# Loading the second copy of batch 0's coordinates on ScalarE's DMA queue, ahead of the mask

## The reference, cut to what matters

```python
def reference(x, ctx_4096, fside, mask, lora_B, router_W, router_b, Wq, ..., ln_b):
    # layer 0, with lora_A = ctx_4096 (4 x 64 x 512)
    w = softmax(x @ router_W.T + router_b)                 # 8 experts
    a_sum = einsum('bsh,arh->bsr', x, ctx_4096)
    x = nan_to_num(x + 0.5 * einsum('bsn,bsnh->bsh', w, einsum('bsr,nhr->bsnh', a_sum, lora_B)))
    # layer 1: x attends to ctx_4096, 32 heads of 16, masked where mask == 0
    Q, K, V = x @ Wq.T + bq, ctx @ Wk.T + bk, ctx @ Wv.T + bv
    x = layernorm(x + softmax(mask(Q K^T / 4)) V @ Wo.T + bo) * ln_g + ln_b
    # layers 2 and 3, the same: xyz = ctx_4096 (b, 64, 512), points = x
    sq = sum(xyz * xyz, axis=1)
    d2 = sq[:, :, None] + sq[:, None, :] - 2.0 * einsum('bdn,bdm->bnm', xyz, xyz)
    idx = top_k(-d2, 8)
    for i in range(4):
        p = leaky_relu(points)
        points = (fside[i] @ p + sum over the 8 neighbours of fside[i] @ p) / 9 + points
    return points
```

## Time and profile before

| | |
|---|---|
| median of 3 runs | 377.51 us (377.25, 377.51, 379.73) |
| the profiled execution, own time | 377.08 us |
| its span, first to last instruction | 375.3 us |
| PE busy | 365.6 us (97%) |
| PE weight loads | 309.9 us (83%) |
| DVE, ACT, POOL busy | 272.7, 176.9, 128.9 us |
| bytes moved by DMA | 22.47 MB |
| granted TensorE clock, mean | 1.000 |

### The profile page before, as it was taken

How to read it: one execution, slowest core, us unless ns; L and a number is a source line. 1 busy time by engine, 2 the same in 40 slices (tenths; PEclk the granted TensorE clock), 3 DMA queues, 4 the chain that set the end, 5 groups by cost and what they waited for, 6 DMA issues and landing times.

```text
span 375.3 us, 6566 instructions
## 1 busy us (share of the span) xinstructions
PE 365.6 (97%) x2396; PEld 309.9 (83%) x2396; DVE 272.7 (73%) x427; ACT 176.9 (47%) x308; POOL 128.9 (34%) x125
## 2 busy tenths in 40 slices
PE   7899999999999999999999999999999999999996
PEld 4677887878878877877898889898989889898895
DVE  4945899997899898579848984567686476565524
ACT  2256457857897586383426162234324233424311
POOL 5059216200501414023344254435427234344320
PEclk9999999999999999999999999999999999999999
DMA  6995127127038507500000000000000000000023
GB/s 198 325 347 164 22 65 186 39 53 161 8 102 190 68 2 149 69 0 3 2 1 0 2 0 2 0 2 1 2 0 2 0 2 0 3 0 2 0 86 140
DMA packets 25056, 22.47 MB, mean 60 GB/s; under 512 B 9537, under 2 KB 20546, under 8 KB 25026
## 3 DMA queue, kind: packets, MB, share of 16 engines
q1 hardware_dynamic: 24352, 22.04, 22.2%
q10 hardware_dynamic: 674, 0.02, 0.1%
HBM read 12.35 MB, written 3.15 MB: 41 GB/s over the span
## 4 chain that ended last, share of the span: by engine, by line
PE 85%; DVE 5%; ACT 4%; DMA 3%; issue 2%; SPq 1%; DVEq 0%; ACTq 0%
PE slot L564 82%; DMA wk<-in_WkT 3%; ACT k_blk_hi L943 2%; PE slot L684 1%; PE slot L693 1%; SPq L448 1%; PE slot L725 1%; ACT probT L976 1%; DVE p_full L1321 1%; DVE points L1331 1%; ACT adj L874 1%; DVE inv_full L1267 0%; ACT L976 0%; DVE stats L1282 0%; DVE shift L1255 0%
## 5 line engine op out<-in xcount | busy, mean ns | idle before, releaser
L1065 POOL TENSOR_TENSOR p_lo<-p_full,p_hi 128x512 fp32r<-128x512 f32 x64 | 86.0, 1361 | 157.1 <-ACT p_hi L1016 157.0
L1026 ACT ACTIVATE u_hi<-slot 128x512 fp32r<-128x512 f32 x64 | 36.1, 593 | 69.3 <-PE slot L564 69.2
L1326 DVE TENSOR_TENSOR u_lo<-slot,u_hi 128x512 fp32r<-128x512 f32 x64 | 42.4, 684 | 31.5 <-ACT u_hi L1026 31.5
L1016 ACT ACTIVATE p_hi<-p_full 128x512 fp32r<-128x512 f32 x64 | 39.0, 627 | 55.3 <-DVE p_full L1321 55.2
L564 PE MATMUL slot<-adj,u_hi 128*128 128x512 f32 x256 | 64.8, 392 | 0.1
L564 PE MATMUL slot<-fs_hi,p_hi 128*128 128x256 f32 x256 | 64.8, 286 | 0.0
L1331 DVE SCALAR_TENSOR_TENSOR points<-slot,points 128x512 f32<-128x512 f32 x64 | 42.7, 684 | 30.4 <-PE slot L564 30.4
L564 PE MATMUL slot<-adj,u_lo 128*128 128x512 f32 x256 | 64.1, 391 | 0.0
L564 PE MATMUL slot<-fs_lo,p_hi 128*128 128x256 f32 x256 | 64.1, 283 | 0.0
L1321 DVE SCALAR_TENSOR_TENSOR p_full<-points 128x512 f32<-128x512 f32 x64 | 54.3, 863 | 8.9 <-POOL p_lo L1065 6.3
L564 PEld LDWEIGHTS slot<-adj,u_lo 128*128 128x128 f32 x256 | 47.5, 188 | 10.1 <-issue 0.4
(11 more groups left out here) (144 smaller groups left out, 567.3 us busy)
## 6 DMA issues: line engine op xcount, KB each, us to landing
q_stack<-q_hi SPq DMA_DIRECT2D x32, 128.0 KB, 2.4
x_in<-in_xT SPq DMA_DIRECT2D x8, 256.0 KB, 4.7
q_stack<-q_lo SPq DMA_DIRECT2D x16, 128.0 KB, 2.5
out_points<-points SPq DMA_DIRECT2D x8, 256.0 KB, 2.0
loraB_raw<-in_lora_BT SPq DMA_DIRECT2D x1, 1024.0 KB, 7.8
wk<-in_WkT SPq DMA_DIRECT2D x1, 1024.0 KB, 10.6
wq_raw<-in_WqT SPq DMA_DIRECT2D x1, 1024.0 KB, 10.4
wv<-in_WvT SPq DMA_DIRECT2D x1, 1024.0 KB, 11.2
```

Source lines behind the costliest of these rows:

```text
L1016: act.activation(p_hi[b][:, (i % 2) * H:(i % 2 + 1) * H], p_full[:, p_buf[b, i]], ACT.Copy)\
L1026: act.activation(half_of(u_hi[:, u], i % 2), bank("wa", b, i // 2, i % 2), ACT.Copy)\
L1065: pool.tensor_tensor(lo[:, cut], full[:, cut], hi[:, cut].bitcast(F32), ALU.subtract)\
L1326: dve.tensor_tensor(half_of(u_lo[:, u], i % 2), bank("wa", b, i // 2, i % 2), half_of(u_hi[:, u], i % 2).bitcast(F32), ALU.subtract).then_ ...
```

## The change

In SP's `load_xyz` the second transfer (into `xyz_n[b]`) is issued only for b >= 1. For batch 0 it is issued by ScalarE, as the first instruction of its program, ahead of the mask row. Bytes, destinations, semaphore and its counts are the same.

```diff
             def load_xyz(b):
                 load(xyz[b][0:V, :], ctx[b], f"xyz{b}")
-                load(xyz_n[b][0:V, :], ctx[b], f"xyz{b}")
+                if b >= 1:
+                    load(xyz_n[b][0:V, :], ctx[b], f"xyz{b}")
...
         @block.scalar
         def _(act):
 
+            act.dma_start(xyz_n[0][0:V, :], ctx[0]).then_inc(loads["xyz0"], 16)
             act.dma_start(mask_row_i[:], mask.rearrange("b v -> (b v)").unsqueeze(0)).then_inc(loads["mask_all"], 16)
```

## The result

The changed kernel takes 381.51 us (median of 6 executions, 381.36 to 382.11), the kernel before 377.53 us (6 executions, 376.82 to 379.73): 1.0101 times as long, 95% interval 1.0079 to 1.0123. The forecast was 376.9 us and no measurable change. It is slower by 4 us, outside the range, which ended at 378.4.

What follows compares the result with a forecast made beforehand. TensorE was taken as the bound, with wk's load deciding when `keys` starts. Terms -0.62 (SP) + 0 + 0 gave -0.6 us on the 377.51 us median: 376.9 us, range 375.9 to 378.4.

Steps and rivals of the forecast that it cites:

- the last bullet of part 3: DMA engines around ctx_t's load: xyz_n and small packets now run beside it; at most 0.6 us, taken as 0.
- Rival B: DMA engines, 2 to 5 us: early transfers collide, up to 0.6 us on wk, 377.8 to 378.1 us; chance 0.09.
- Part 1: SP's queue: one issue fewer, so ctx_t and wk issue 0.62 us earlier; wk's landing taken to follow by 0.6 us.
- Part 2: Start of `keys` on TensorE: other inputs leave 2.16 and 1.04 us, so the 0.6 us reaches the end whole.
- the rest of part 3: ScalarE's queue: one more issue delays mask row, router's weights, bias and first instruction by 0.57 us, at no cost.
- Rival C: Head of TensorE's list: mask row landing after about 5.5 us delays the kernel, up to 383.9 us; chance 0.02.

## Why the prediction was wrong, point by point

**The step that failed is the last bullet of part 3,** the small packets beside ctx_t. I bounded them by 0.6 us, took 0, and argued from unused engine share. The term measured 2.7 us on wk (17.28 with the bias, 14.59 without), over four times my bound, and through the clock another 1.7 us on `keys`. I priced the pieces by their bytes, 20 KB, and called the low windows from 3 to 6 us room that nobody used. They were in part the mark of the bias: issued at 1.78, it was in flight until 5.5, at the place where the rates were lowest; without it these windows fill in part, and the run with two copies stretches them. Low share beside megabytes of issued work was here a symptom, not a reserve: even where the windows filled, in the kernel before without its bias, wk came no sooner.

**Rival B had the place nearly right** (pieces of ScalarE's queue beside SP's stream, though from 6 to 10 us and not from 2 to 5) and the price wrong by a factor of four, so that even it ended at 378.1 us. It named the router's pieces; the 512 of its weights are not needed for the loss, the 128 of its bias are. Its point of decision, wk later than 14.86, was the right thing to look at.

**The clock is a step that I left out.** I read 1.00 in the windows of one execution and took it as given. It had held over an idle time of 1.28 us that is enough to lose it now and then: 28 of 102 executions of the kernel before, beside the experiments, ran at a mean clock of 0.995. Any delay of wk makes that time longer, and so each further wait had to be priced with the chance of 1.7 us on top. The term measured 1.69 us in the profiled execution.

**Part 1, issue and landing.** SP's issues did move as forecast, though by 0.41 us at wk and not 0.62: with both engines issuing 128 KB loads, ctx_t's issue took 0.81 us where it had taken 0.60. The landing follows only where the bias is out of the way: 14.3 with the bias first, 14.59 without the bias, 14.71 with it behind wk, against 14.86. With the coordinates last, 15.0. The strict reading of the Trainium skill ("DMA: Bandwidth & Descriptors", section "Issuing engines are not separate DMA queues"), that another issuing engine saves the sequencer's time and no more, is nearer to this than my sum was; that it can cost 2.4 us it does not say.

**Part 2, the cover, was overstated.** `keys` also waits for `near0_0` to free its bank, at 14.16 in the kernel before (13.48 + 0.68): 0.70 us of room before wk and not 1.04. I had looked at the two engines that feed `keys` and not at who holds its bank. A gain of 0.6 would still have passed, as `near0_0` too hangs on ctx_t. That what happens at the head reaches the end was right: 4.11 us at 17 us, 4.4 at the end.

**Of the rest of part 3, the times of use held and some landings did not.** ScalarE's queue was later by 0.60 us at the mask and 0.92 us at the bias, not by 0.57 throughout, and the router's weights landed at 7.0 and its bias at 10.4, not before 6.1; both were still there before they were used. The squares were computed at 4.54 (forecast 4.5), the mask row was used at 4.06 (2.7 to 5.1), VectorE began on ctx_t at 6.84 (7.0), and none of these cost anything. Rival C did not occur in the changed kernel and did with the bias first.

**What stays open.** From 2 to 14 us the engines moved 300 GB/s before and 283 after:

```profile
2.00:14.00 12.00, 11.11 (x30) 6.00 (x29) 7.61 (x17) 2.29 (x3) 4.25 (x18) 1.00 0.93 300
```

```profile
2.00:14.00 12.00, 11.55 (x30) 5.96 (x29) 7.91 (x18) 2.29 (x3) 4.34 (x18) 1.00 0.90 283
```

That is 17 GB/s over 12 us, about 0.2 MB or half a microsecond of full rate, and yet wk is 2.4 us later. From 2 us to wk's landing the engines moved 292 GB/s over 12.86 us before, 3.76 MB, and 273 GB/s over 15.28 us after, 4.17 MB: 0.4 MB more had gone by when wk was there. It looks as if other loads behind wk went ahead on some engines while wk was unfinished on others; the profile's views don't separate the 16 engines, so I can't show which. Why the collision is full in some executions and small in others is open as well. And why the pieces from one place hold up the other queue is argued only: the Trainium skill ("DMA: Bandwidth & Descriptors", section "Queues, rings and completion order") says that each engine alternates between the queues for which it has work; slow reads on one would then hold back the other. No run here shows the alternation itself.

## What to carry to other kernels

Count a transfer's pieces and where they read, not its bytes: a 4 KB load spread from one place over 128 rows can hold back a megabyte stream, so try it behind what is needed first (here 377.61 us) or ahead of the stream (here 378.52 us, because it delayed the mask), and moving anything in front of it moves it too. Where the engines' share is low although much is issued, ask who is in flight before you call it room. And where TensorE idles ahead of a late load, look at the mean clock of every execution, not only at the profiled one.

## What the runs showed of the hardware

- 128 pieces of 32 bytes from one place, landing: 2.7 us as first load, 3.7 us in the kernel before, 4.9 us there with SP's loads sooner (coordinates last), 5.3 us with the small loads later and SP untouched, 6.3 us as a second copy, 6.1 to 7.7 us with both (4.3 us in one execution). From 128 rows: 4.8 us.
- With them in flight, the engines moved 151 to 199 GB/s from 6 to 9 us in the changed kernel, without them 333 to 359 in the same microseconds; with two copies 97 to 178 from 5 to 8 us. Not in all of their flight: 245 and 280 GB/s from 4 to 6 us in the changed kernel.
- SP's issue of the two 128 KB loads behind wk took 3.0 to 4.1 us in the five profiled executions in which wk landed at 16.8 or later, and 1.1 to 2.2 us in the twelve others: the issuing queue shows the hold-up.
- TensorE's clock fell to 0.50 after idle times of 1.9, 2.1, 2.4, 3.6 and 3.6 us in profiled executions, and held after 1.1, 1.2, 1.3, 1.5, 1.9, 2.0 and 2.6 us: between, both happen. The kernel before, with 1.28 us in its profile, lost it in 28 of its 102 executions beside the experiments. A fall cost 1.5 to 1.7 us in `keys` and 3.0 us in one execution (11.87 against 8.87), and 1.8 to 2.3 us between the medians of the two groups.
- Two engines that issue loads of 128 KB at the same time: the issue behind them took 0.81 us on SP and 0.76 us for 1 KB on ScalarE, against 0.60 and 0.50 us.
